# Causal mask of the first attention: the second pair of units masked by predicated copies on VectorE

## The reference

```python
xq, xk, xv = (x @ Wq), (x @ Wk), (x @ Wv)      # 32 query heads, 8 key heads, 16 features each
xq, xk = apply_rotary_emb(xq), apply_rotary_emb(xk)
scores = einsum('bqhd,bkhd->bhqk', xq, repeat(xk, 4)) / sqrt(16)
scores = where(causal, scores, -inf)            # 64 x 64, lower triangle kept
probs  = softmax(scores)
out    = einsum('bhqk,bkhd->bqhd', probs, repeat(xv, 4)) @ Wo
```

## Time and profile before

| what | value |
|---|---|
| median of 3 runs | 766.34 us (765.5 to 769.43) |
| the profiled execution's own time | 764.84 us |
| its span | 763.0 us |
| PE busy | 738.5 us, 97% of the span |
| DVE busy | 514.5 us, 67% |
| ACT busy | 276.1 us, 36% |
| POOL busy | 370.0 us, 48% |
| first attention | from about 17 us to about 165 us of the span |
| PE's granted clock | 0.996 of full speed |

### The profile page before, as it was taken

The page is one execution under the profiler, slowest core; times in us unless marked ns, Lnnn a source line. Parts: engine busy times, 40 slices in busy tenths (PEclk is TensorE's granted clock), DMA queues, the critical chain, the costliest instruction groups (busy, mean ns, idle before and its releaser), DMA issues.

```text
span 763.0 us, 13142 instructions
## 1 busy us (share of the span) xinstructions
PE 738.5 (97%) x4649; PEld 632.4 (83%) x4649; DVE 514.5 (67%) x997; ACT 276.1 (36%) x604; POOL 370.0 (48%) x368
## 2 busy tenths in 40 slices
PE   6899999899999999999999999999999999999996
PEld 4688888888888888888888888888888888888874
DVE  4789999767665756665675567566656655577777
ACT  4656666523232322322232223223232322133425
POOL 7667666835444444434463444445344634352204
PEclk9999999999999999999999999999999999999999
DMA  7810040223433233222222232322232223240002
GB/s 195 216 35 18 17 127 4 60 70 98 111 83 70 63 83 90 56 55 82 55 55 55 82 73 62 86 81 55 55 82 55 56 56 83 50 115 3 1 1 110
DMA packets 107875, 53.54 MB, mean 70 GB/s; under 512 B 80449, under 2 KB 96961, under 8 KB 107841
## 3 DMA queue, kind: packets, MB, share of 16 engines
q1 hardware_dynamic: 107008, 51.51, 26.6%
q10 hardware_dynamic: 576, 1.05, 0.4%
q0 software_dynamic: 256, 0.52, 0.3%
HBM read 32.62 MB, written 2.10 MB: 46 GB/s over the span
## 4 chain that ended last, share of the span: by engine, by line
PE 89%; POOL 4%; DVE 3%; issue 2%; ACT 1%; DMA 0%; POOLq 0%; SPq 0%; DVEq 0%; ACTq 0%
PE bank L781 23%; PE bank L717 22%; PE bank L519 15%; PE s_bank L793 7%; PE bank L543 3%; PE bank L765 2%; PE bank L572 2%; PE bank L939 2%; PE s_bank L765 1%; DVE arena_r L1670 1%; POOL arena_f L1442 1%; PE s_bank L623 1%; POOL arena_f L1437 1%; PE bank L774 1%; PE bank L748 1%
## 5 line engine op out<-in xcount | busy, mean ns | idle before, releaser
L781 PE MATMUL bank<-arena_r 128*128 128x512 f32 x768 | 192.0, 399 | 0.0
L717 PE MATMUL bank<-arena_r 128*128 128x512 f32 x720 | 185.3, 400 | 0.5 <-DVE arena_r L1670 0.5
L1048 ACT ACTIVATE arena_r<-bank 128x256 fp32r<-128x256 f32 (+2 forms) x201 | 87.7, 460 | 217.1 <-PE bank L748 105.8
L781 PEld LDWEIGHTS bank<-arena_r 128*128 128x128 f32 x768 | 139.6, 188 | 27.5
L717 PEld LDWEIGHTS bank<-arena_r 128*128 128x128 f32 x720 | 130.7, 188 | 29.6 <-DVE arena_r L1670 0.8
L519 PE MATMUL bank<-arena_r 128*128 128x256 f32 (+1 forms) x1056 | 147.2, 294 | 1.2 <-DVE arena_r L1670 0.8
L519 PEld LDWEIGHTS bank<-arena_r 128*128 128x128 f32 x1056 | 137.4, 191 | 8.0 <-DVE arena_r L1670 1.1
L1670 DVE TENSOR_TENSOR arena_r<-bank,arena_r 128x256 fp32r<-128x256 f32 (+2 forms) x201 | 99.4, 514 | 47.0 <-ACT arena_r L1048 46.3
L1511 POOL TENSOR_TENSOR arena_f<-arena_f 128x512 f32<-128x512 f32 x30 | 39.2, 1305 | 110.2 <-DVE arena_f L1862 110.2
L1911 DVE COPY_PREDICATED arena_f<-mask_i,small 128x512 f32<-128x512 int32 x32 | 41.7, 1303 | 52.0 <-ACT arena_f L1048 52.0
L1879 DVE TENSOR_TENSOR arena_f<-bank,arena_f 128x512 f32<-128x512 f32 x64 | 43.9, 686 | 42.7 <-PE bank L781 42.5
(11 more groups left out here) (163 smaller groups left out, 1048.1 us busy)
## 6 DMA issues: line engine op xcount, KB each, us to landing
arena_f<-arena_f SPq DMA_DIRECT2D x120, 128.0 KB, 2.5
arena_f<-in_L_xattn_Wo SPq DMA_DIRECT2D x8, 1024.0 KB, 5.6
arena_f<-in_L_xattn_Wq SPq DMA_DIRECT2D x14, 512.0 KB, 4.0
arena_f<-in_x SPq DMA_DIRECT2D x8, 256.0 KB
arena_f<-in_x SPq DMA_DIRECT2D x1, 2048.0 KB, 9.5
arena_f<-in_L_xattn_Wk SPq DMA_DIRECT2D x8, 256.0 KB, 3.0
arena_f<-in_L_xattn_Wv SPq DMA_DIRECT2D x8, 256.0 KB, 3.3
arena_f<-in_ctx SPq DMA_DIRECT2D x8, 256.0 KB, 3.1
```

Source lines behind the costliest of these rows:

```text
L717: mm = pe.matmul(BQ2[f][:], w2q_s[a][:, e, j, f, :], xT[b][:, e, tok], start=(e == 0 and n == 0), stop=(e == EC - 1 and n == 2))
L781: mm = pe.matmul(BO2[i][:], at2[a][:, h, i * P:(i + 1) * P], w2o_s[b][:, h, :], start=(h == 0 and n == 0), stop=(h == HG - 1 and n == 2))
L1048: act.activation(dst, src, ACT.Copy).then_inc(done, 1)
```

## The change

The constant matmul L613 is issued for the pair (0, 1) only. In the pair (2, 3) the first score matmul starts the bank's accumulation instead. ACT no longer copies units 2 and 3. DVE does it in `largest`, with a predicated copy from the bank to `sc1[u % 2]`, where the mask `causal` (128 x 64, repeated over the 8 blocks) is one. At the other places `sc1[u % 2]` keeps what it held: the -2**120 that unit u - 2 of the same tile left there.

```diff
@@ PE, s_stage
-                for u in units:
+                for u in units if even == 0 else ():
                     rows = slice(S * (u % 2), S * (u % 2) + S)
                     pe.matmul(SB[u % 2], rows_q[rows].rearrange("p j q -> p (j q)"),
                               bars[rows].rearrange("p x k -> p (x k)"), start=True, stop=False,
...
-                                           start=False, stop=(n == 2), skip_group_check=True)
+                                           start=(even == 2 and n == 0), stop=(n == 2), skip_group_check=True)
@@ ACT, scores_copy1
-                if u >= 2 or not first:
+                if not first:
@@ ACT, tile_steps, last tile
-                    scores_copy1(i, 2, False)
-                    scores_copy1(i, 3, False)
@@ ACT, tile_steps, other tiles
                 expo(i, 0)
-                scores_copy1(i, 2, not old)
                 if oldest:
                     x1_keep(w)
                 expo(i, 1)
-                scores_copy1(i, 3, not old)
@@ DVE
             def largest(v, u):
+                if u >= 2:
+                    dve.wait_ge(s_s, 4 * v + u + 1)
+                    dve.wait_ge(s_sub, 4 * v + u - 1)
+                    hold()
+                    dve.copy_predicated(cut(sc1[u % 2], b=8, k=S), bcast(causal[:], 1, 8),
+                                        cut(banks[5 + u % 2][:], b=8, k=S)).then_inc(s_cp, 1)
                 dve.wait_ge(s_cp, 4 * v + u + 1)
                 dve.tensor_reduce(mx1[u], cut(sc1[u % 2], b=8, k=S), AX.X, ALU.max).then_inc(s_mx, 1)
```

## The result

The changed kernel takes 772.66 us (median of 4 runs, 771.23 to 774.04), the kernel before 766.19 us on the same chip (median of 4): +6.5 us, a ratio of 1.008 with a 95% interval of 1.006 to 1.010. Forecast were 770.9 us and +4.6. The profiled execution has a span of 772.2 us against 763.0, 9.2 us more. That is more than the 6.5 us of the medians, because the profiled execution of the changed kernel is the slowest of its four (774.04 us) and that of the kernel before one of the quickest (764.84 us).

What follows compares the result with a forecast made beforehand. PE (14.97 of 15 us busy) bounds the steady tiles, DVE (14.07) close behind. Terms 4.65 + 0.79 - 0.83 = +4.6 us, on the 766.34 us median 770.9 us; own range 768.5 to 773, over all cases 766.3 to 778.9.

Steps and rivals of the forecast that it cites:

- Whatever makes L1698 late makes PE's `k_turns` late: Steady tiles: delay of DVE's rotary key product delays PE's key transposes and the next tile; engines within 0.15 us there.
- The slack is 0.74 us: Steady tiles, ahead of DVE's key product L1698: it could come at 77.02 but came at 77.76, leaving 0.74 us free.
- 0.78 per copy, 0.11 for `hold()`, 1.67 per tile: DVE's added work ahead of L1698: two predicated copies of 0.78 us with hand-over, plus 0.11 for one `hold()`.
- Tiles 2 to 6: 4.65: Five steady tiles each pay 1.67 added less 0.74 slack, 0.93 us, together 4.65 us more.
- Tile 7: -0.83: Last tile: DVE copies in its 3.06 us hole, and POOL's waits of 0.30 and 0.53 go, giving back 0.83 us.
- Copies hidden from POOL: DVE's copies read data from PSUM, so POOL shouldn't delay them; the rival, collision, had chance 0.12, +12.5 us, 778.8 us.
- I add nothing: DVE's new copies: the skill's PSUM penalty, 0.065 us each, 0.9 us over 14, was left out because the trace disagreed.
- PE loses 0.33 us, which doesn't count: Steady tiles: dropping L613 for the second pair frees PE 0.33 us per tile, worth nothing since PE waits at `k_turns`.
- Tiles 0 and 1 pay 0.40 and 0.39: First two tiles: slack of 1.27 and 1.28 us against 1.67 added leaves 0.40 and 0.39, together 0.79 us.
- the faster case: Rival, chance 0.08: PE remains last and each tile gains its 0.33 us, the last 0.83; 3.14 us less, 763.2 us.
- partly absorbed: Rival, chance 0.25: waits shift together, half a microsecond per steady tile, nothing in tiles 0 and 1; +1.7, 768.0 us.
- PE stays last: Rival, chance 0.08: DVE hides both copies in the 0.74 us ahead of L1698, so the kernel gets faster, 763.2 us.

Runs made afterwards that it cites:

- e5: The kernel before with DVE making the predicated copy of unit 3 alone, ACT still copying unit 2, mask matmul kept for both: 770.59 us, ratio 1.0039.
- e4: The kernel before with the change made in the last tile alone: ratio 0.9976, 764.57 us.
- e6: The changed kernel with ACT copying units 2 and 3 to SBUF, so DVE's predicated copy reads mask and data there: 783.25 us, ratio 1.0205.
- e1: The changed kernel with the constant mask matmul run for the second pair too, DVE still copying: 772.88 us, ratio 1.0075.
- e2: The kernel before without the mask matmul of the second pair, ACT still copying: 765.39 us, ratio 0.9978.
- e9: The changed kernel with matmuls for nothing in the first steps (3, 6, 4) and in tile 0's waits (6, 3): 768.35 us, ratio 1.0022.
- e10: The kernel before with matmuls for nothing in the first steps (3, 6, 4) and in tile 0's waits (6, 2): 763.80 us, ratio 0.9964.
- e3: The changed kernel with 6 and 3 matmuls for nothing ahead of the third and fourth transposes of tile 0: 770.53 us, ratio 1.0048.
- e7: The kernel before with matmuls for nothing in the waits of its first steps (3, 6, 4): 764.82 us, ratio 0.9975.

## Why the prediction was right, and where it was not

- **"Whatever makes L1698 late makes PE's `k_turns` late"**: right in size, but the way that counts is the other one. The chain moved from PE to DVE, and PE waits 0.85 us in the tile shown. It waits in `pt_stage(1)`, for POOL's `norm(1)`, and `k_turns` follows without a wait. The forecast named this place for the wait, but took its slack from L1698 alone.
- **"The slack is 0.74 us"**: e5 bears it out, where one copy of 0.78 us cost 0.03 us per tile. That it also holds for the way through `norm(1)` is luck. In the changed kernel `pt_stage(1)` starts 85.96 - 84.49 = 1.47 us behind DVE's second reciprocal and `k_turns` 0.49 us later. Counted from 76.30 that gives 78.26, against 79.06 for `k_turns` before: 0.80 us. In tile 0 the two ways differ.
- **"0.78 per copy, 0.11 for `hold()`, 1.67 per tile"**: measured 0.78 and 0.79, and 1.69 between the two reciprocals. In front of unit 2's copy stand 80.40 - 80.16 = 0.24 us instead of the plain 0.12: 0.12 for the 0.11.
- **"Tiles 2 to 6: 4.65"**: 4.57. **"Tile 7: -0.83"**: -0.91, and e4 has it alone.
- **"Copies hidden from POOL"**: right. The rule of the Trainium skill that a VectorE instruction contends with a GpSimd instruction reading SBUF only when it has two SBUF inputs (SBUF — State Buffer, "Who interferes with whom") fits the predicated copies too (e6). The prediction says that the rows agree with both halves for a subtraction. For the first half its rows show a predicated copy; a subtraction with both inputs in SBUF and a POOL instruction beside it is elsewhere in the trace before, with 1.69 us, where one with nothing beside it takes 0.68 (at 134.54 us):

```profile
253.14 1.69 DVE L1670 TENSOR_TENSOR arena_r<-arena_f,arena_r 128x512 fp32r<-128x512 f32 x1
```

- **"I add nothing" for the PSUM source**: right. The Trainium skill (VectorE: DVE Perf Modes, the table under the errata) gives a PSUM source more time than one in SBUF, and no run here shows it: the new copies take 0.744 and 0.755 us in the median, those of the second attention with all in SBUF 0.74 when nothing is beside them.
- **"PE loses 0.33 us, which doesn't count"**: right, by e1. The size was a little high: alone it is worth 0.24 per steady tile (e2), since the matmul behind it then takes 0.10 us more.
- **"Tiles 0 and 1 pay 0.40 and 0.39"**: the terms that were mis-sized. In the profiled execution they paid 2.73 and 2.29. Two steps failed.
  - *The slack of tile 0.* The forecast took 1.27 us, ahead of L1698. On the way through `norm(1)` only 0.67 us were free, and at full clock tile 0 pays 1.01 (e9 against e10). For tile 1 the term holds: 0.35 (e3) and 0.32 (e9).
  - *PE's clock.* The sum has no term for it and takes PE's waits as free wherever DVE is last. The granted clock in 36 to 44 us went from 1.00 to 0.59. With matmuls in PE's waits of tile 0 it stays full there (e3), and with matmuls in the first steps too it stays full throughout (e9). The profile before had shown the danger: 0.79 in 18 to 26 us, in the same tile. The change at full clock costs 4.55 us by e9 and e10, forecast 4.6; the measured 6.5 us hold about 1.9 us on top, which go with the clock.
- **The size of the whole** came out right, slower and within the forecast's own range of 768.5 to 773, since the five steady tiles and the last one make up most of it. There is luck in it. The median of 772.66 is close to the upper end, and two of the four runs (773.16 and 774.04) lie beyond it. At full clock the 0.6 us that tile 0 pays above its forecast are mostly made up for elsewhere, by steady tiles of 0.88 instead of 0.93 and by 0.91 instead of 0.83 in the last. The range "over all cases", 766.3 to 778.9, leaves out two times that the prediction itself works out: 763.2 for the faster case, and 782.0 (766.34 + 15.7) for copies of 1.57 us.
- "DVE over 96% busy" was a little high: 14.22 of 15 us, 95%. The rivals "partly absorbed" and "PE stays last" fell with the steady tiles' 0.91 us.

Not settled: why the clock falls near 20 us for longer in the profiled execution of the changed kernel. That start was 0.52 us later, before anything in the change had run, and the stretch differs from run to run. Nor is it shown that the change's own waits bring on the second fall. The profiled executions of e2, with no predicated copy, and of e5, with one per tile, have both falls, with PE idle in tile 0 for 4.7 and 4.5 us against 4.8 before and 5.6 in the changed kernel. What is shown is that matmuls in the waits take the falls away in nearly every run, and that low clocks are common in the changed kernel (three runs of four at 0.989) and rare in the one before (9 of 71 at 0.989 or 0.990).

## What to carry to other kernels

When work moves to an engine that is 93% busy beside a bound of 100%, don't compare shares: find the place in the tile where its idle time lies, and count only what is added ahead of that place beyond the slack there. Do this for every engine that waits for something behind the added work: the smallest slack counts, and in tile 0 it was not the one next to DVE's own wait. Then look where the engine that used to be last will wait now; if that is TensorE, and it waits in a stretch where it was half idle already, its clock may fall for the microseconds that follow. A few matmuls for nothing in such waits made no tile longer here and were worth 1.9 us (e7) and 2.8 us (e10) by the medians. And a change that loses in seven tiles can be kept for the one tile that has a hole for it.

## What the runs showed of the hardware

- A predicated copy of 128 x 512 floats with an int32 mask takes VectorE 0.74 to 0.76 us, from PSUM with POOL working beside it, and 0.83 to 1.32 us (median 1.18) when mask and data both lie in SBUF.
- The time of a run follows PE's mean clock closely: in e5, 765.7 us at 0.995, 768.4 at 0.990, 771 at 0.986. In the changed kernel the clock fell at about 36 us; from 32 to 36 us PE was busy for 1.68 us. With PE busy for 3.47 us of them (e3) it stayed full. The busy time of this stretch does not decide it alone: in e4, whose clock had been low only briefly around 20 us, it stayed full after 1.82 us, and in e1 it fell in the stretch itself, with PE busy for 1.99 us.
